# Scores of three attention phases as matmuls on 32 rows of each head, without masked queries

## What is computed

```python
# third block, twice: self attention (256 keys), then cross attention (512 keys)
scores = jnp.einsum('bhqd,bhkd->bhqk', q, k) * HD ** (-0.5)   # HEADS 16, HD 8
p = jax.nn.softmax(scores, axis=-1)
o = jnp.einsum('bhqk,bhkd->bhqd', p, v)
# fourth block (512 keys)
logits = jnp.einsum('bqhd,bkhd->bhqk', q, k) * scale          # HEAD_DIM 8
attn = jax.nn.softmax(logits, axis=-1)
```

## Time and profile before

| | |
|---|---|
| median of 3 runs | 2450.96 us (2449.66 to 2453.04) |
| span of the profiled execution | 2444.4 us |
| TensorE matmuls (PE), busy | 1928.4 us, 79% |
| TensorE weight loads (PEld) | 1500.6 us, 61% |
| VectorE (DVE) | 1548.4 us, 63% |
| ScalarE (ACT) | 1378.6 us, 56% |
| GpSimd (POOL) | 230.4 us, 9% |
| mean granted TensorE clock | 0.928 of 2.4 GHz |
| HBM traffic | 5 GB/s over the span |

### The profile page before, as it was taken

One profiled execution on the slowest core, in us unless ns is written; L12 is line 12 of the kernel. 1 busy time (PEld: TensorE's weight loads), 2 busy tenths in 40 slices (PEclk: granted clock), 3 DMA queues, 4 the chain that ended last, 5 costly groups with the idle time before them and its releaser, 6 DMA issues. The chain is left out here.

```text
span 2444.4 us, 40943 instructions
## 1 busy us (share of the span) xinstructions
PE 1928.4 (79%) x14064; PEld 1500.6 (61%) x14064; DVE 1548.4 (63%) x3455; ACT 1378.6 (56%) x3682; POOL 230.4 (9%) x489
## 2 busy tenths in 40 slices
PE   1899876777689987777678998778778898867777
PEld 1777665555477765555557776566556776656554
DVE  2667567775367665777546756677656665667764
ACT  1556555766355654666545555467655555546664
POOL 0000012111000001210100000111110000011111
PEclk7999998989899999898889999889889999989998
DMA  5000000000000000000000000000000000000000
GB/s 127 7 1 1 1 1 1 1 1 1 17 1 1 1 1 1 1 1 1 8 10 1 1 1 1 1 1 1 1 8 9 1 1 1 1 1 1 1 1 5
DMA packets 24322, 13.84 MB, mean 6 GB/s; under 512 B 9296, under 2 KB 23632, under 8 KB 24112
## 3 DMA queue, kind: packets, MB, share of 16 engines
q1 hardware_dynamic: 24112, 11.11, 1.9%
HBM read 10.06 MB, written 1.05 MB: 5 GB/s over the span
## 5 line engine op out<-in xcount | busy, mean ns | idle before, releaser
L989 ACT ACTIVATE probs<-scores,nmax 128x512 f32<-128x512 f32 (+1 forms) x1024 | 587.4, 580 | 171.4 <-DVE nmax L1386 168.9
L1386 DVE TENSOR_REDUCE nmax<-scores 128x1 f32<-128x512 f32 (+1 forms) x768 | 520.0, 684 | 119.7 <-PE scores L401 73.4
L469 PE MATMUL turned<-ident,probs 128*128 128x128 f32 x3072 | 496.9, 287 | 74.3 <-ACT probs L989 71.7
L469 PEld LDWEIGHTS turned<-ident,probs 128*128 128x128 f32 x3072 | 378.8, 146 | 166.1 <-ACT probs L989 120.1
L757 PE MATMUL heads_out<-probs_t,v 128*32 128x256 f32 (+1 forms) x4096 | 377.4, 412 | 9.5 <-issue 5.2
L823 ACT ACTIVATE probs_t<-turned 128x512 f32<-128x512 f32 x384 | 229.5, 598 | 100.1 <-PE turned L469 94.1
L1399 DVE COPY probs_t<-turned 128x512 f32<-128x512 f32 x384 | 261.9, 682 | 26.4 <-PE turned L469 26.3
L757 PEld LDWEIGHTS heads_out<-probs_t,v 128*32 128x32 f32 (+1 forms) x4096 | 185.6, 127 | 135.6 <-issue 55.2
L724 PE MATMUL scores<-k_t,q_mask 128*128 128x256 f32 (+1 forms) x512 | 192.4, 423 | 75.5 <-POOL q_mask L1524 37.1
L1411 DVE TENSOR_TENSOR out_t<-heads_out,scale_t 128x256 f32<-128x256 f32 x192 | 81.6, 425 | 260.0 <-ACT scale_t L823 260.0
L1524 POOL CAST q_mask<-q_t 32x256 fp32r<-32x256 f32 x384 | 157.2, 409 | 657.5 <-PE scores L724 222.5
(11 more groups left out here) (307 smaller groups left out, 3342.1 us busy)
## 6 DMA issues: line engine op xcount, KB each, us to landing
out_t<-ctx_dram SPq DMA_DIRECT2D x8, 192.0 KB, 2.5
v<-wqt_dram SPq DMA_DIRECT2D x2, 512.0 KB, 5.0
wo<-wo_dram SPq DMA_DIRECT2D x2, 512.0 KB, 5.6
x<-x_dram SPq DMA_DIRECT2D x8, 128.0 KB, 2.4
y_dram<-x SPq DMA_DIRECT2D x8, 128.0 KB, 1.8
v<-wkt_dram SPq DMA_DIRECT2D x1, 512.0 KB, 5.0
probs_t<-wv_dram SPq DMA_DIRECT2D x1, 512.0 KB, 6.3
wff<-wff_dram SPq DMA_DIRECT2D x1, 512.0 KB, 5.8
```

What stands on the lines that cost most here:

```text
L469: return nc.tensor.transpose(out, in_, ident[:, :])
L989: last = nc.scalar.activation(probs[:, n % 3, k * S:k * S + ph.keys], bank[:, k * S:k * S + ph.keys], ACT.Exp, bias=nmax[:, h * QB + qb:h ...
L1386: nc.vector.tensor_reduce(out, src, AX.X, ALU.max, negate=True).then_inc(sem["attention_max"], 1)
```

## The change

The masked copies of the queries go. A score matmul now reads the 32 partitions of its head from `q_t` and `k_t` themselves, so that it contracts over 32 rows of the array instead of 128. The number of matmuls, their columns and their outputs stay as they were. `q_mask`, its memset, GpSimd's 384 copies, their semaphore and TensorE's wait for it go with them. The waits for `qt0` and `qt1`, which GpSimd had at the start of a phase, are now TensorE's, and in cross2 and l3 it waits for `kt0` and `kt1` too.

```diff
-                if ph.masked:
-                    pe.wait_ge(sem["attention_mask"], ph.at("mask", h + 1))
-                else:
+                if not ph.masked:
                     pe.wait_ge(sem["attention_t_lo"], ph.at("t_lo", h + 1))
+                rows = slice(32 * (h % 4), 32 * (h % 4) + 32)
                 bank = SC[ph.at("scores", u) % 3]
                 if ph.key_major:
                     for k in range(2):
                         kb = 2 * part + k
-                        last = nc.tensor.matmul(bank[:, k * S:(k + 1) * S], k_t[s][:, h // 4, kb * P:(kb + 1) * P],
-                                                q_mask[:, h % 4, :], start=True, stop=True)
+                        last = nc.tensor.matmul(bank[:, k * S:(k + 1) * S],
+                                                k_t[s][rows, h // 4, kb * P:(kb + 1) * P],
+                                                q_t[s][rows, h // 4, :], start=True, stop=True)
...
                         if ph.masked:
-                            last = nc.tensor.matmul(out, q_mask[:, h % 4, q], k_t[s][:, h // 4, 0:ph.keys],
+                            last = nc.tensor.matmul(out, q_t[s][rows, h // 4, q], k_t[s][rows, h // 4, 0:ph.keys],
                                                     start=True, stop=True)
...
-                                   "self2": ("mid1", ("kt0", "kt1")), "cross2": ("mid2", ("kt2", "kt3")),
-                                   "l3": ("mid3", ("kt2", "kt3"))}[ph.name]
+                                   "self2": ("mid1", ("qt0", "qt1", "kt0", "kt1")),
+                                   "cross2": ("mid2", ("qt0", "qt1", "kt0", "kt1", "kt2", "kt3")),
+                                   "l3": ("mid3", ("qt0", "qt1", "kt0", "kt1", "kt2", "kt3"))}[ph.name]
...
-            nc.gpsimd.memset(f32(q_mask[:, :, :]), 0.0)
...
-                if issued["attention_mask"]:
-                    pool.wait_ge(sem["attention_mask"], issued["attention_mask"])
...
-            def mask(ph, h):
-
-                g, i = h // 4, h % 4
-                if h >= 4:
-                    pool.wait_ge(sem["attention_scores"], ph.at("scores", (h - 3) * ph.per_head))
...
-                nc.gpsimd.tensor_copy(q_mask[rows, i, :], f32(q_t[ph.s][rows, g, :])
-                                      ).then_inc(sem["attention_mask"], 1)
```

More of the change, by code:

```diff
@@ L68, in counts @@
         qm = 0 if self.key_major else 1
-        return {"t": t, "t_hi": t, "t_lo": t, "mask": H if self.masked else 0, "scores": self.units,
+        return {"t": t, "t_hi": t, "t_lo": t, "scores": self.units,
                 "max": self.units * qm, "exp": self.units, "turned": self.units * qm,
@@ L356, in program @@
         scale_t = sb("scale_t", [P, 2, S])
-        q_mask = sb("q_mask", [P, 4, S], F32R)
         table_probe = sb("table_probe", [P, 2])
@@ L1479, in _ @@
             setup_end(pool)
-            issued = {"attention_mask": 0, "rstd": 0, "pads": 0}
+            issued = {"rstd": 0, "pads": 0}
             def power(key, blocks=QB):
-                if issued["attention_mask"]:
-                    pool.wait_ge(sem["attention_mask"], issued["attention_mask"])
                 if issued["pads"]:
@@ L1511, in chain @@
                         issued["pads"] += 2
-            def mask(ph, h):
-                g, i = h // 4, h % 4
-                if h >= 4:
-                    pool.wait_ge(sem["attention_scores"], ph.at("scores", (h - 3) * ph.per_head))
-                if issued["rstd"]:
-                    pool.wait_ge(sem["rstd"], issued["rstd"])
-                if issued["pads"]:
-                    pool.wait_ge(sem["pads"], issued["pads"])
-                issued["attention_mask"] += 1
-                rows = slice(32 * i, 32 * i + 32)
-                nc.gpsimd.tensor_copy(q_mask[rows, i, :], f32(q_t[ph.s][rows, g, :])
-                                      ).then_inc(sem["attention_mask"], 1)
-            def attention(ph):
-                if ph.masked:
-                    name = {"self2": "mid1", "cross2": "mid2", "l3": "mid3"}[ph.name]
-                    if precedes((name, ph.s), (ph.name, ph.s)):
-                        pool.wait_ge(sem[bank_read((name, ph.s, "qt0"))], FILL[name, ph.s, "qt0"])
-                        pool.wait_ge(sem[bank_read((name, ph.s, "qt1"))], FILL[name, ph.s, "qt1"])
-                    if ph.before["scores"]:
-                        pool.wait_ge(sem["attention_scores"], ph.at("scores", 0))
-                    for h in range(3 // ph.per_head + 1):
-                        mask(ph, h)
+            def attention(ph):
                 yield
                 for u in range(ph.units):
-                    if u > 0 and ph.masked and (u + 3) % ph.per_head == 0 and (u + 3) // ph.per_head < H:
-                        mask(ph, (u + 3) // ph.per_head)
                     yield
@@ L1544, in segment @@
                 enter(name)
-                issued.update(attention_mask=0, rstd=0, pads=0)
+                issued.update(rstd=0, pads=0)
                 run_rounds(name, attention, chain)
```

## The result

The changed kernel takes 2569.11 us in the median of 4 runs (2566.07 to 2577.65), beside 2450.31 us for the kernel before in the same series: a ratio of 1.0479, 95% interval 1.0452 to 1.0506. The forecast was 2478 us, 1.1% slower; it is 4.8% slower, beyond the range. The profiled execution spans 2564.3 us, 119.9 more than before. Its mean granted clock is 0.877 of 2.4 GHz, where it was 0.928.

A forecast was written before the change was run, and what follows sets the result against it. No engine was full; the touched phases were taken as bound by a chain passing between engines. 2444.4 - 12 - 8 + 47 = 2471.4, with 6.6 us around the span 2478 us; range 2462 to 2500, with rivals 2430 to 2518.

The forecast's parts named there:

- The masks, forecast -20 us: Removing GpSimd's mask copies gains 12 us from TensorE's mask waits and 8 us from VectorE working beside GpSimd.
- Rows change shape as columns do: At score groups on TensorE, 32-row matmuls pay like column-tiled head outputs: 0.20 us entering, 0.15 us leaving the narrow shape.
- The rival without a price for rows: Row changes at the scores cost nothing, leaving only the gains: 2431 us, between 2394 and 2451; chance 0.22.
- 430 entries and 330 exits: Closely spaced shape changes counted on TensorE in cross2, self2 and l3, adding 136 us of its time.
- 35% of it on the path: Of the 136 us added to TensorE in the touched phases, 35% lengthens the run: 47 us, bounds 0 and 136.
- The clock: Thinner TensorE work in the touched phases brings 1.2 GHz more often: 32 us more, 2510 us; chance 0.13.
- The sign that the forecast named: TensorE's granted clock (PEclk) under 0.85 in the touched phases' windows would show that the clock rival holds.
- 64 us of longer transposes and scores: On TensorE, 0.6 us more for one unit in six at 1.2 GHz; half of it taken as on the path.
- the waits ahead of a fall are gone: Argument against the clock rival: the waits that went before a fall of TensorE's clock disappear; no size given.

The follow-up runs named there:

- rows128: The changed kernel with each score matmul reading all 128 rows, still without masks (scores summed over four heads): 2435.72 us, ratio 0.9938.
- rows96: The changed kernel with score matmuls over 96 rows instead of 32 (scores of three heads summed): 2447.88 us, ratio 0.9990.
- rows64: The changed kernel with score matmuls over 64 rows instead of 32 (scores of two heads summed): 2540.05 us, ratio 1.0390.
- tiny32half: rows128 with one extra 32-row, 8-column matmul ahead of the score group at every second unit only: 2474.50 us.
- tiny32: rows128 with one extra 32-row, 8-column matmul ahead of every score group, the scores staying at full width: 2564.70 us.
- pairs32: The changed kernel with two units' scores issued together in self2 and cross2, halving the changes of shape there: 2591.28 us, ratio 1.0570.
- fill_after: The changed kernel with one more full-width 512-column matmul for each unit of the three touched phases: 2680.79 us, ratio 1.0940.
- tiny128: rows128 with one extra 8-column matmul on all 128 rows ahead of every score group, without a change of shape: 2467.32 us.

## Why the prediction was wrong

Its direction was right, and the changes of shape do cost more than the masks did. It gave +47 us for the changes, where they and what comes with them cost 133 (2569.1 less the 2435.7 of rows128). Point by point:

- **The masks, forecast -20 us.** Measured -14 (rows128). The waits for masks are gone and a normalised block takes 343 ns in the median after, over the whole execution, as it did only without masks beside it. This step holds.
- **Rows change shape as columns do, 0.20 us in and 0.15 out.** Measured 0.19 and 0.15 at 2.4 GHz. The rival without a price for rows falls: rows96 streams, rows64 doesn't. This agrees with the Trainium skill, "TensorEngine Tiling (Array Packing)", Key Properties, where a change of the tiling mode, not of the tile, drains TensorE; the price stands in no page and is the one measured here.
- **430 entries and 330 exits.** In the trace after there are 442 and 392 tight ones: more exits are tight because fewer transposes still wait for their exponentials (76.9 us against 120.1). At 2.4 GHz this is 143 us of TensorE's time, and some 155 with the higher price at 1.2 GHz for the fifth of them that fall there, not 136. A small error.
- **35% of it on the path, 47 us.** As an average it holds, by the estimate below: 47 of 143 us, a third. tiny32half and tiny32 give a third and two fifths, pairs32 about 30%. Part of this is luck. The share isn't a constant: it was read from a kernel with more room on TensorE, and on top of the changed kernel it is over half (fill_after). By its own shares of 25 to 50% the range should start at 2465 us, not 2462; it changes nothing.
- **The clock, put at nothing in the sum and held apart as a rival with 0.13. This is the step that failed.** The sum has no term for it, and the rival, which had one, took 32 us. It isn't a rival but a second term, which comes with the first. From rows128 to the changed kernel the mean time at 1.2 GHz went from 368 to 645 us, 277 more, and at 0.31 us for each that is some 86 of the 133 us. The sign that the forecast named, under 0.85 in these windows, is there: 0.83, 0.82 and 0.74. The rival alone would have been short too, at 2510: it took half of 64 us of longer transposes and scores. What the forecast held against the rival, that the waits ahead of a fall are gone, didn't protect the clock either, since it now also falls behind work (last section). And taking those waits away gave little: rows128, which has none, has a mean low time of 368 us, beside 375 before.

The 133 us, then, are some 86 for the clock and 47 for the changes. This is an estimate. It rests on the price of 0.31 holding for 277 us, where the runs of one kernel that give it differ by at most some 110. With the changed kernel's own 0.35 it is 97 and 36; with 0.22, just under the lowest single series, 61 and 72. So the clock's term is some 60 to 100 us where the sum has none, and the changes' term some 35 to 70 where it has 47. rows64 gives the same division: 104 us, of which 179 x 0.31 = 56 for the clock and 48 for the same changes. The sum would have been

- 2444.4 - 14 + 47 + 86 = 2563 us of span, where it is 2564.3; this closes because the terms come from the same runs, and tests nothing.

By phase the profiled runs say where it went (after less rows128: time, then low time): cross2 63 us and 92, l3 39 and 120, self2 19 and 24. l3 has the fewest changes and the most added low time.

Still open: why the clock is low for longer. Mean low time goes with rows in use (368, 406, 547 and 645 us for 128, 96, 64 and 32), the first step of it without a change of shape but within the spread of the runs; it goes with the changes too (376 to 469 from tiny128 to tiny32 with full-width scores). No kernel here has 32-row scores without changes. What the masks' waits and VectorE beside GpSimd each gave of the 14 us is open as well.

## What to carry to other kernels

A share of the path that is read from a profile prices busy time that is added to an engine. It doesn't hold what the change does to TensorE's clock, and here that was the larger part. Two readings would have shown a part of this before the change was made. One is the price of low time: several runs of the kernel as it is, their granted clocks against their times. The other is a kernel with the new instruction form and a part of the computation left out, whose granted clock is then read.

The share itself is that of a small addition. Here it stayed near a third for some 140 us on an engine with 23 to 28% of idle time, and was over half for what came on top. A filler shows this, if it is the same work in both kernels: between narrow matmuls a full-width filler adds changes of shape.

In these phases the 32-row matmuls saved nothing on TensorE, since only rows were dropped. Two shapes in turn cost 0.34 us for each round trip, which has to be bought with something; freeing an idle engine wasn't it. Long runs of narrow matmuls would have fewer changes; pairs32, with half of them in two phases, lost 23 us to them by the estimate and not 47, but 49 us to its order. Narrow matmuls side by side in different rows were not tried.

## What the runs showed of the hardware

- 96 rows stream with full-width matmuls around them and 64 and 32 don't. A unit of cross2 with 96 rows goes through in 0.68 us, one with 32 in 1.01, and the medians of 64 rows are those of 32.
- Time at 1.2 GHz costs about a third of itself in this kernel: 0.31 us for each, over 125 runs.
- A change of shape costs more at 1.2 GHz, but not twice: 0.29 and 0.19 us against 0.19 and 0.15.
- In the changed kernel the clock stayed low through stretches of full work. Before there are 64 stretches at 1.2 GHz after the setup, of 5.0 us in the mean; after, 72 of 8.3 us. So it doesn't fall much more often, it comes back later. The stretch from 1112.6 to 1126.2 of the changed kernel, columns as in the earlier trace rows, has TensorE busy without a gap by its modelled ends, in turns of 32-row scores and 128x128 transposes and then head outputs, and the clock at 0.50 throughout:

```profile
1109.20:1112.60 3.40, 1.98 (x9) 1.33 (x10) 2.50 (x5) 1.50 (x4) 0.00 (x0) 0.91 0.00 0
1112.60:1116.00 3.40, 3.40 (x13) 2.30 (x11) 1.64 (x3) 1.84 (x6) 0.00 (x0) 0.50 0.00 0
...
1122.80:1126.20 3.40, 3.40 (x21) 1.72 (x25) 1.10 (x3) 1.86 (x4) 0.00 (x0) 0.50 0.00 0
```

- It also fell with work before it: at 1231.5 us in l3 of the changed kernel, columns the same:

```profile
1228.00:1231.50 3.50, 3.20 (x21) 2.45 (x20) 3.43 (x5) 1.70 (x4) 0.00 (x0) 0.99 0.00 0
1231.50:1235.00 3.50, 3.48 (x26) 2.04 (x29) 3.38 (x6) 1.85 (x4) 0.00 (x0) 0.50 0.00 0
```

In the kernel before the falls come behind waits: over the 2 us ahead of a fall TensorE stood idle for 69% of the time in the mean, and it was busy for over 70% of them at 1 of 64 falls. In the changed kernel it stood idle for 56%, and was that busy at 25 of 72.

- Full-width work put into room on TensorE raised the clock: with the filler in the kernel before, cross2 stood at 0.99 rather than 0.93, and took no longer.
